# A 16-block transformer kernel on one core: the last stage's first pair of tiles is prepared inside the stage before it

## The chip, the cores and the metric

One core of a Trainium2 chip runs the whole program. The metric is device time in microseconds (us) of one execution; the time before is the median of three runs. The engines are TensorE (PE in the profile, its weight loads PEld), VectorE (DVE), ScalarE (ACT), GpSimd (POOL) and SyncE (SP), which issues most of the DMAs. Each engine works through its own instructions in order, and they meet at semaphores.

## What is computed

The input x is 16 batches of 128 tokens with 256 features. Eight layers update it one after the other; the two that matter here are the last two:

```
x = x + tanh(g_xattn[3]) * L3_xattn(layernorm(x), ctx, ctx)
x = x + tanh(g_ffn[3])   * L3_ffn(layernorm(x))

L3_xattn(Q, K, V):   # per batch, Q, K, V are 128 x 256
    score = sigmoid(Q.T @ K / sqrt(128))      # 256 x 256
    return V @ score

L3_ffn(x):           # router, 8 experts (2 chosen for each token), and a shared part of width 1024
    shared = (silu(x @ sw1.T) * (x @ sw2.T)) @ sw3.T
    scores = sigmoid(x @ router_w.T); the two best of scores + expert_bias, their scores normed to sum 1
    routed = sum over the two of weight * expert(x)
    return shared + routed
```

## The kernel before

x stays in SBUF as `x[:, b]`, b = 0 to 15, a tile of 128 tokens by 256 features each. The program has stages 0 to 7, one for each layer. An engine goes to stage s when `stage_over(eng, s)` lets it: it waits until stage s - 1 has made its last update of x. Stages 2, 4 and 6 count their updates in the semaphore `x_done`, so stage 7 begins when `x_done` has 16 more counts than at the start of stage 6.

**Stage 6** (attention, `s6_dve`, `s6_act`, `s6_pe`, `s6_sp`) has one turn for each tile b. DVE normalises tile b + 2 (`norm`, lines 739, 742, 747; POOL computes the reciprocal deviation between them, lines 755 and 757), subtracts for the low half of a piece of the last stage's weights (`w7l`, line 2770), and updates x (line 2772). PE does the scores of tile b + 1 (line 2796) and then the output of tile b (line 2806). ACT does the sigmoid (line 2782) and the high half of the weights' piece (`w7h`, line 2785). SP loads rows, context and weights two turns ahead. `pipeline` writes the turns out: for DVE, which looks two ahead, turn 0, a hardware loop over turns 1 to 12, and turns 13, 14 and 15 written out; for PE, one ahead, turn 15 alone behind the loop; ACT and POOL have all turns in a loop. In DVE's turns 14 and 15 and in PE's turn 15 nothing is left to normalise or score.

**Stage 7** (feed-forward, `s7_pe`, `s7_act`, `s7_dve`, `s7_pool`) works in pairs of tiles. For each of the 8 pairs b the shared part has 8 units j: PE does `up(b, j)`, 12 matmuls (lines 1665 to 1667), ACT a silu (line 1742), DVE the product (line 1760), and later `down`. Ahead of its units each pair needs a front: `pair_stats` (DVE, lines 1321 and 1325), `pair_rstd` (POOL, lines 755 and 757), `pair_apply` (DVE, line 747, out `xnD`), `pair_transpose` (PE, line 1655, into bank 0), `ff_front_act` (ACT, lines 1342 and 1344: `xnT` and its rounded form `xnTh`), `low_x` (DVE, line 1423: the rest `xnTl`), `pair_logits` (PE, line 1530) and `pair_logits_copy` (DVE, line 1539). The front of pair b + 1 lies between the units of pair b. The front of pair 0 has no units before it: all of it stands ahead of the loop, behind `stage_over(7)`. Routed tokens are written to DRAM by POOL's indirect DMAs, in slots that count the `h` products; after pair 3 come the experts' tiles (`tiles_pe` and its fellows), then pairs 4 to 7.

Of the kernel before, what the change touches and what calls it, by code (L numbers as in the profile page):

```python
# [69 lines left out]
def bass_program(nc, a, out, n_stages=8):  # L70
# [5 lines left out]
    with ctx:  # L76
# [1382 lines left out]
        def pair_xn(n):  # L1459
            return xnD[:, n] if n < HALF else xn[:, n % 2]  # L1460

        def way_pos(n):
            return WAY_PAIRS.index(n)

# [177 lines left out]
        def s7_pe(pe):  # L1642
            F = lambda n: f[7, n]
            MM = nc.tensor.matmul
            UP, DOWN = TOP_E * UNIT, TOP_E * UNIT + 4096

            def pair_transpose(n):
                pe.wait_ge(F("xn").sem, F("xn").at(2 * n + 1, 1))
                if n == 1:
                    pe.wait_ge(F("lg").sem, F("lg").at(0, 1))  # L1650
                elif 2 <= n <= HALF:
                    pe.wait_ge(R7.sem, R7.at((0, 1, 3)[n - 2], 15))
                for c in range(NC):
                    for u in range(2):
                        o = nc.tensor.transpose(bank(0)[:, 256 * c + 128 * u:256 * c + 128 * (u + 1)], pair_xn(n)[:, u, 128 * c:128 * (c + 1)], ident[:])
                o.then_inc(F("xnT_psum").sem, 1)

            def up(b, j):
                pe.wait_ge(F("h").sem, F("h").at(b, j - UP_RING + 1))
                for v in range(2):  # L1660
                    o = bank(2 + j % UP_RING)[:, 256 * v:256 * (v + 1)]
                    for c in range(NC):
                        k = UP + 512 * j + 256 * c + 128 * v
                        wh, wl = w7h[:, k:k + 128], w7l[:, k:k + 128]
                        MM(o, wh, xnTh[:, b % 2, c], start=(c == 0), stop=False)  # L1665
                        MM(o, wh, xnTl[:, b % 2, c], start=False, stop=False)  # L1666
                        t = MM(o, wl, xnTh[:, b % 2, c], start=False, stop=(c == NC - 1))  # L1667
                t.then_inc(F("up").sem, 1)

            def down(b, i):  # L1670
                pe.wait_ge(F("hl").sem, F("hl").at(b, i + 1))
                if i == 0:
                    pe.wait_ge(F("acc").sem, F("acc").at(b, -1))
                k = DOWN + C * i
                wh, wl = w7h[:, k:k + C], w7l[:, k:k + C]
                for u in range(2):
                    o = bank(6 + b % 2)[:, C * u:C * (u + 1)]
                    hh, hl = (h[:, i % 4, T * u:T * (u + 1)] for h in (hTh, hTl))
                    MM(o, hh, wh, start=(i == 0 and u == 0), stop=False, skip_group_check=True)
                    MM(o, hh, wl, start=False, stop=False, skip_group_check=True)  # L1680
                    t = MM(o, hl, wh, start=False, stop=(i == 7), skip_group_check=True)
                t.then_inc(F("y").sem, 1)

            def fronts(b, j):
                n = b + 1
                if n < NB // 2 and j == (5 if n == HALF else 2):
                    pair_transpose(n)
                if n < HALF and j == 3:
                    pair_logits(pe, n)
                if (b, j) in WAY_TRANSPOSE:  # L1690
                    way_transpose(pe, WAY_TRANSPOSE[b, j])
                if (b, j) in WAY_LOGITS:
                    way_logits(pe, WAY_LOGITS[b, j])
                if (b, j) in PLACES:
                    group_places(pe, PLACES[b, j])
                if (b, j) == (3, 4):
                    group_count_pe(pe)

            pair_transpose(0)
            pair_logits(pe, 0)  # L1700
            for b in range(NB // 2):
                pe.wait_ge(F("xnT").sem, F("xnT").at(b, 1))
                pe.wait_ge(F("xnTl").sem, F("xnTl").at(b, 1))
                for j in range(8):
                    up(b, j)
                    if j >= DISTANCE:
                        down(b, j - DISTANCE)
                    elif b % HALF:
                        down(b - 1, 8 - DISTANCE + j)
                    fronts(b, j)  # L1710
                if b % HALF == HALF - 1:
                    for i in range(8 - DISTANCE, 8):
                        down(b, i)
                if b == HALF - 1:
                    tiles_pe(pe, L7)
                    for fl in (L7.t_low, L7.u_h, L7.h_low, L7.d_out):
                        pe.wait_ge(fl.sem, fl.at(N_TILES, 0))

        def s7_act(act):
# [14 lines left out]
                if (b, j) in TANH:  # L1734
                    group_tanh(act, TANH[b, j])

            ff_front_act(7, act, 0, 0)
            for b in range(NB // 2):
                for j in range(8):
                    act.wait_ge(F("up").sem, F("up").at(b, j + 1))  # L1740
# [12 lines left out]
        def s7_dve(dve):  # L1753
# [16 lines left out]
                V.scalar_tensor_tensor(x[:, 2 * p:2 * p + 2], bank(6 + p % 2).rearrange("p (u c) -> p u c", u=2), gates[:, 7:8], x[:, 2 * p:2 * p + 2],  # L1770
                                       ALU.mult, ALU.add).then_inc(F("acc").sem, 1)

            def pair_stats(n):
                ff_stats(7, dve, n, n % 2)

            def pair_apply(n):
                for u in range(2):
                    ln_apply(7, dve, 2 * n + u, 2 * (n % 2) + u, pair_xn(n)[:, u])

            COMBINE = {}  # L1780
            for t in range(NB):
                slot = 8 * HALF + 4 + 8 * t // 5
# [2 lines left out]
            def fronts(b, j):  # L1785
                n = b + 1
                if (b, j) in PAIR_STATS:
                    pair_stats(PAIR_STATS[b, j])
                if n < NB // 2 and j == (4 if n == HALF else 1):
                    pair_apply(n)  # L1790
                if (b, j) in WAY_STATS:
                    way_stats(dve, WAY_STATS[b, j])
                if n < NB // 2 and j == (6 if n == HALF else 3):
# [13 lines left out]
                for t in COMBINE.get((b, j), ()):  # L1807
                    combine7(dve, t)

            pair_stats(0)  # L1810
            pair_apply(0)
            low_x(7, dve, 0, 0)
            pair_logits_copy(dve, 0)
            for b in range(NB // 2):
# [13 lines left out]
                    tiles_dve(dve, L7)  # L1828

        def s7_pool(pool):  # L1830
            rs = rstd_step(7, pool)

            def pair_rstd(n):
                for u in range(2):
                    rs(2 * n + u, 2 * (n % 2) + u)

            pair_rstd(0)
            pair_rstd(1)
            way_rstd(pool, 4)
            way_rstd(pool, 5)  # L1840
            pair_rstd(2)
            group_scatter(pool, 0, (0, 1), SCATTER_AT[0])
            way_rstd(pool, 6)
            group_scatter(pool, 0, (2, 3), SCATTER_AT[0])
            way_rstd(pool, 7)
            pair_rstd(3)
            group_scatter(pool, 1, range(4), SCATTER_AT[1])
            group_scatter(pool, 2, range(4), SCATTER_AT[2])
            pair_rstd(4)
            group_scatter(pool, 3)  # L1850
            for k in range(3):
                pool.wait_ge(y_out[k], L7.stored(N_TILES // 3))
            pool.wait_ge(table_ready, 2 * (TABLE_STEPS + RESULT_STEPS))
            for t in range(NB):
                if t in (1, 7, 12):
                    pair_rstd({1: 5, 7: 6, 12: 7}[t])
                gather(pool, t, got7, combined7)

        def tiles_sp(sp, L):
# [894 lines left out]
        def s6_dve(dve):  # L2754
            F = lambda n: f[6, n]

            def norm(b, s):
                ln_stats(6, dve, b, None, s)
                ln_apply(6, dve, b, s, xn[:, s, 0])

            def first():
                norm(0, 0)
                norm(1, 1)

            def body(p, b, n, s, turn, turn_b):
                if n is not None:
                    dve.wait_ge(F("s_psum").sem, F("s_psum").at(b, 1))
                    norm(n, s)
                dve.wait_ge(F("w7_high").sem, F("w7_high").at(b, 1))
                nc.vector.tensor_tensor(w7l[:, bass.ds(b * W7C, W7C)], w7_raw[:, s], w7h[:, bass.ds(b * W7C, W7C)].bitcast(F32), ALU.subtract).then_inc(F("w7_low").sem, 1)  # L2770
                dve.wait_ge(F("y").sem, F("y").at(b, 1))
                nc.vector.scalar_tensor_tensor(x[:, b], bank(4 + s)[:, 0:C], gates[:, 3:4], x[:, b], ALU.mult, ALU.add).then_inc(x_done.sem, 1)

            pipeline(dve, first, body, lambda p, s: None, ahead=2)

# [11 lines left out]
        def s6_pe(pe):  # L2787
# [11 lines left out]
            def body(p, b, n, s, turn, turn_b):  # L2799
                if n is not None:  # L2800
                    scores(n, 1 - s, turn)
                pe.wait_ge(F(f"ctx_loaded{s}").sem, F(f"ctx_loaded{s}").at(turn_b, 16))
                pe.wait_ge(F("s").sem, F("s").at(b, 1))
                pe.wait_ge(x_done.sem, b + (3 * NB - 1))
# [1 line left out]
                    t = MM(bank(4 + s)[:, 0:C], ctxT[:, s, n], sgm[:, s, n], start=(n == 0), stop=(n == 1))  # L2806
                t.then_inc(F("y").sem, 1)

            pipeline(pe, lambda: scores(0, 0, 0), body, lambda p, s: None)

        c_in = [sem("c_in0"), sem("c_in1")]
# [70 lines left out]
        def _(act):  # L2883
# [14 lines left out]
            for s, prog in enumerate((None, lambda: tiles_act(act, L1), lambda: s2_act(act), lambda: s3_act(act), lambda: s4_act(act),  # L2898
                                      lambda: s5_act(act), lambda: s6_act(act), lambda: s7_act(act))):
                if 0 < s < n_stages:  # L2900
                    stage_over(act, s)
                    if s == 1:
                        act.wait_ge(loaded_later, LOADS_1)
# [60 lines left out]
        def _(pool):  # L2964
# [19 lines left out]
            fetch(0, 0)  # L2984
            fetch(1, 1)
            for s in range(1, n_stages):
                stage_over(pool, s)
                if s == 1:
                    s1_pool(pool, ctx_split(pool, fetch), bias_split, bias_rows)
# [170 lines left out]
```

## Time and profile before

| what | us |
|---|---|
| median of 3 runs | 1343.7 |
| lowest and highest run | 1342.25, 1351.01 |
| the profiled execution | 1340.98 |
| its span, first to last instruction | 1339.2 |
| mean granted TensorE clock | 0.931 of full |

Stage 6 runs from about 1030.8 to 1089.45 on the clock of the profiled span. All times of single instructions below are on that clock. The profiled execution is 1.8 us longer than its span and 2.7 us shorter than the median.

### The profile page before, as it was taken

To read this page: it belongs to the slowest core of one execution; us is meant where nothing else is said; L and a number is where in the kernel's file an instruction comes from. 1 tells how busy PE (TensorE), PEld (TensorE's weight loads), DVE (VectorE), ACT (ScalarE), POOL (GpSimd) and SP (SyncE) were. 2 spreads that over 40 slices of the span, in tenths; PEclk is the share of its full clock that TensorE was granted. 3 is DMA by queue.
4 is the path that set the end of the run, shared out by engine and by line. 5 is a ranking of instruction groups with operands and counts; after the bars stand their busy time and mean duration, and the time that the engine had idled before them with its cause. 6 is when DMAs were issued, how large, how long until landed. Compare 5 with 4: busy or idle time off the path is not lost.

```text
span 1339.2 us, 32909 instructions
## 1 busy us (share of the span) xinstructions
PE 1083.3 (81%) x11717; PEld 832.2 (62%) x11717; DVE 853.1 (64%) x2361; ACT 542.5 (41%) x1049; POOL 507.0 (38%) x1023
## 2 busy tenths in 40 slices
PE   4889898885676588887998799999856569989898
PEld 2566666664575244445666567666644449878798
DVE  2665566565454698975666577777756656555475
ACT  2455454554453477662000132323211644346533
POOL 2444554454884888711001111111313214520261
PEclk8898999898798599998999899999868989989999
DMA  5332223501575455421000000000010630124331
GB/s 181 122 112 69 96 89 127 179 18 36 163 215 178 129 148 145 129 90 64 1 0 0 24 25 16 24 16 23 0 40 4 177 94 32 65 95 152 115 106 64
DMA packets 105784, 112.61 MB, mean 84 GB/s; under 512 B 12548, under 2 KB 95636, under 8 KB 104892
## 3 DMA queue, kind: packets, MB, share of 16 engines
q1 hardware_dynamic: 96732, 88.47, 21.1%
q0 software_dynamic: 8064, 22.06, 5.4%
q8 instruction: 78, 1.28, 0.4%
q10 hardware_dynamic: 864, 0.43, 0.1%
q14 instruction: 46, 0.38, 0.1%
HBM read 66.07 MB, written 44.84 MB: 83 GB/s over the span
## 4 chain that ended last, share of the span: by engine, by line
PE 54%; DVE 17%; issue 10%; ACT 6%; DMA 6%; POOL 3%; SPq 1%; another core or an unknown queue 1%; DVEq 1%; ACTq 0%; POOLq 0%
PE psum L2640 5%; DMA PT<-xs 4%; PE psum L1082 3%; PE psum L2395 2%; DVE mx L852 2%; PE psum L1667 2%; PE psum L1665 2%; ACT ext L2347 2%; PE psum L1666 2%; ACT PT L2338 2%; PE psum L1065 2%; PE psum L1014 2%; PE psum L2380 1%; PE psum L1045 1%; DVE mx L2532 1%
## 5 line engine op out<-in xcount | busy, mean ns | idle before, releaser
L755 POOL TENSOR_SCALAR veps<-mv 128x1 f32<-128x1 f32 x112 | 27.0, 241 | 494.9 <-DVE mv L742 324.8
L852 DVE TENSOR_REDUCE mx<-psum 128x6 f32<-128x960 f32 (+3 forms) x80 | 80.7, 1008 | 77.3 <-PE psum L1050 62.5
L733 POOL DMA_INDIRECT got<-ys,rows_y x64 | 63.9, 999 | 117.9 <-DMA ys<-yt 91.7
L939 ACT ACTIVATE PT<-psum 128x1024 f32<-128x1024 f32 x64 | 65.6, 1025 | 76.6 <-PE psum L1070 76.5
L2298 DVE TENSOR_REDUCE mx<-psum 128x4 f32<-128x1024 f32 x64 | 77.0, 1206 | 19.7 <-PE psum L2369 18.7
L2338 ACT ACTIVATE PT<-psum 128x1024 f32<-128x1024 f32 x64 | 65.5, 1024 | 36.4 <-PE psum L2380 34.7
L1665 PE MATMUL psum<-xnTh,w7h 128*128 128x256 f32 x256 | 76.0, 297 | 1.9 <-issue 1.9
L2640 PE MATMUL psum<-mskp,ident_r 128*128 128x512 f32 x256 | 71.2, 414 | 7.5 <-DVE mx L2532 6.4
L2109 DVE SCALAR_TENSOR_TENSOR x<-psum,cw,x 128x256 f32 (+1 forms) x128 | 53.0, 476 | 36.2 <-PE psum L2057 35.9
L1666 PE MATMUL psum<-xnTl,w7h 128*128 128x256 f32 x256 | 74.0, 289 | 0.6 <-issue 0.6
L1667 PE MATMUL psum<-xnTh,w7l 128*128 128x256 f32 x256 | 73.9, 289 | 0.0
L2395 PE MATMUL psum<-PT,arena 128*32 128x256 f32 x1024 | 70.1, 388 | 0.1
L757 POOL TENSOR_TENSOR rstd<-veps,minus_half 128x1 f32<-128x1 f32 x112 | 64.2, 573 | 9.3
L2592 ACT ACTIVATE PT<-psum 128x1024 f32<-128x1024 f32 x32 | 32.9, 1032 | 84.2 <-PE psum L2705 84.2
L1742 ACT ACTIVATE sil<-psum 128x256 f32<-128x256 f32 x64 | 24.7, 386 | 94.6 <-PE psum L1667 81.7
L2054 PE MATMUL psum<-w3h,xnTh 128*128 128x512 f32 x128 | 62.8, 490 | 0.0
L1760 DVE TENSOR_TENSOR hTf<-sil,psum 128x256 f32<-128x256 f32 x64 | 26.8, 418 | 55.1 <-ACT sil L1742 41.2
L2640 PEld LDWEIGHTS psum<-mskp,ident_r 128*128 128x128 f32 x256 | 44.7, 189 | 27.1 <-DVE mx L2532 16.5
L747 DVE TENSOR_SCALAR xn<-x,mv,rstd 128x256 f32 (+1 forms) x88 | 38.0, 440 | 33.9 <-POOL rstd L757 33.8
L1895 PE MATMUL psum<-ident,PT 128*128 128x128 f32 x156 | 33.4, 297 | 26.9 <-DMA PT<-xs 25.7
L2007 DVE TENSOR_TENSOR ht<-silt,psum 128x128 f32<-128x128 f32 x78 | 22.4, 288 | 45.9 <-ACT silt L1977 45.9
L2055 PE MATMUL psum<-w3l,xnTh 128*128 128x512 f32 x128 | 51.5, 403 | 0.0
(412 smaller groups left out, 3425.6 us busy)
## 6 DMA issues: line engine op xcount, KB each, us to landing
xs<-qpad SPq DMA_DIRECT2D x17, 1024.0 KB
PT<-xs SPq DMA_DIRECT2D x78, 128.0 KB, 2.1
ys<-yt SPq DMA_DIRECT2D x78, 128.0 KB, 2.2
ctxT<-in_ctxT SPq DMA_DIRECT2D x48, 128.0 KB
ext<-qscr SPq DMA_DIRECT2D x96, 64.0 KB
w_raw<-in_w SPq DMA_DIRECT2D x16, 384.0 KB, 3.4
arena<-in_w SPq DMA_DIRECT2D x4, 1280.0 KB, 10.0
q_parts<-kscr SPq DMA_DIRECT2D x66, 64.0 KB
```

Of the source, the lines that this page charges most:

```text
L733: pool.indirect_dma_start(out=dst[:, t % 4, k], out_offset=None, in_=ys[:], in_offset=bass.IndirectOffsetOnAxis(ap=rows_y[:, t, k:k + 1], ...
L757: nc.gpsimd.tensor_tensor(rstd[:, s], veps[:, s], minus_half[:], ALU.pow).then_inc(F("rstd").sem, 1)
L852: V.tensor_reduce(mx0[:, u0:u0 + m].rearrange("p j e -> p e j"), src, axis=AX.X, op=ALU.max, negate=True).then_inc(F("mx").sem, 1)
L939: A.activation(PT[:, 1024 * r:1024 * (r + 1)], bank(6, 2), ACT.Exp).then_inc(F("p").sem, 1)
L1665: MM(o, wh, xnTh[:, b % 2, c], start=(c == 0), stop=False)
L1666: MM(o, wh, xnTl[:, b % 2, c], start=False, stop=False)
L1667: t = MM(o, wl, xnTh[:, b % 2, c], start=False, stop=(c == NC - 1))
L2054: MM(o, xh, wh, start=(c == 0), stop=False)
L2298: V.tensor_reduce(mx2[:, k // 2, 4 * (k % 2):4 * (k % 2) + 4], bank(4 - 4 * (k % 2), 2).rearrange("p (h l) -> p h l", h=4), axis=AX.X, op= ...
L2338: nc.scalar.activation(PT[:, 1024 * k:1024 * (k + 1)], bank(6, 2), ACT.Exp, scale=0.25).then_inc(F("p").sem, 1)
L2395: t = MM(bank(2 + s)[32 * m:32 * (m + 1), C * what:C * (what + 1)], g, PT[:, 1024 * k + 256 * m:1024 * k + 256 * (m + 1)], start=(k == 0 a ...
L2640: MM(bank(4 + r), ident_r[:], mskp[:, s, which, part].unsqueeze(1).to_broadcast([128, 4, T]), start=(part == 0), stop=False, skip_group_ch ...
```

## The change

The front of pair 0 moves into the last turns of stage 6, all but `low_x` and `pair_logits_copy`, which stay where they were.

- DVE: `pair_stats(0)` behind the x update of turn 13; `pair_apply(0)` at the head of turn 14.
- POOL: `pair_rstd(0)` ahead of `stage_over(7)`.
- PE: `pair_transpose(0)` at the head of turn 15, ahead of that turn's output matmuls; `pair_logits(0)` behind them, ahead of `stage_over(7)`.
- ACT: `ff_front_act(7, 0, 0)` ahead of `stage_over(7)`.
- The small statistics buffers of stage 7 change sides, so that pair 0 has slots 2 and 3 of the four, where stage 6 uses 0 and 1: slot (n + 1) % 2 in place of n % 2.

```
+        def pair_slot(n):
+            return (n + 1) % 2
+
+        def pair_stats(dve, n):
+            ff_stats(7, dve, n, pair_slot(n))
...
# s7_pe
-            pair_transpose(0)
-            pair_logits(pe, 0)
# s7_act
-            ff_front_act(7, act, 0, 0)
# s7_dve
-            pair_stats(0)
-            pair_apply(0)
             low_x(7, dve, 0, 0)
             pair_logits_copy(dve, 0)
# s7_pool
-            pair_rstd(0)
-            pair_rstd(1)
+            pair_rstd(pool, 1)
...
# s6_dve, body
                     norm(n, s)
+                if n_stages > 7 and isinstance(b, int) and b == NB - 2:
+                    pair_apply(dve, 0)
                 dve.wait_ge(F("w7_high").sem, F("w7_high").at(b, 1))
...
                 nc.vector.scalar_tensor_tensor(x[:, b], bank(4 + s)[:, 0:C], gates[:, 3:4], x[:, b], ALU.mult, ALU.add).then_inc(x_done.sem, 1)
+                if n_stages > 7 and isinstance(b, int) and b == NB - 3:
+                    dve.wait_ge(x_done.sem, 3 * NB + 2)
+                    pair_stats(dve, 0)
# s6_pe, body
                 if n is not None:
                     scores(n, 1 - s, turn)
+                elif n_stages > 7:
+                    pair_transpose(pe, 0)
...
-            pipeline(pe, lambda: scores(0, 0, 0), body, lambda p, s: None)
+            pipeline(pe, lambda: scores(0, 0, 0), body, lambda p, s: None if n_stages == 7 else pair_logits(pe, 0))
# ACT's block
                 if 0 < s < n_stages:
+                    if s == 7:
+                        ff_front_act(7, act, 0, 0)
                     stage_over(act, s)
# POOL's block
+                if s == 7:
+                    pair_rstd(pool, 0)
                 stage_over(pool, s)
```

## Rows read from the trace of the kernel before

**Rows 1.** The page: busy time by engine, and the chain that ended last by engine.
```profile
PE 1083.3 (81%) x11717; PEld 832.2 (62%) x11717; DVE 853.1 (64%) x2361; ACT 542.5 (41%) x1049; POOL 507.0 (38%) x1023
...
PE 54%; DVE 17%; issue 10%; ACT 6%; DMA 6%; POOL 3%; SPq 1%; another core or an unknown queue 1%; DVEq 1%; ACTq 0%; POOLq 0%
```

**Rows 2.** Windows (length; busy PE, PEld, DVE, ACT, POOL; clock; DMA): stage 6, gap.
```profile
1030.80:1089.45 58.65, 34.50 (x128) 24.84 (x128) 35.56 (x80) 32.90 (x40) 12.45 (x32) 0.94 0.53 157
1089.45:1097.10 7.65, 2.75 (x12) 2.38 (x13) 2.53 (x7) 2.36 (x3) 1.56 (x4) 0.56 0.00 1
```

**Rows 3.** Timeline of stage 6's turns 13 to 15: start, us, engine, what.
```profile
1082.78 0.95 DVE L2770 TENSOR_TENSOR w7l<-w_raw,w7h 128x768 fp32r<-128x768 f32 x1
1083.65 0.48 DVE L2772 SCALAR_TENSOR_TENSOR x<-psum,gates,x 128x256 f32<-128x256 f32 x1
...
1084.96 0.96 DVE L2770 TENSOR_TENSOR w7l<-w_raw,w7h 128x768 fp32r<-128x768 f32 x1 [0.83 <-ACT w7h L2785]
...
1086.85 0.48 DVE L2772 SCALAR_TENSOR_TENSOR x<-psum,gates,x 128x256 f32<-128x256 f32 x1 [0.94 <-PE psum L2806]
1087.22 0.83 ACT L2785 CAST w7h<-w_raw 128x768 f32 x1 [0.64 <-DMA w_raw<-in_w]
...
1087.49 1.13 PE L2806 MATMUL psum<-PT,ctxT 128*128 128x256 f32 x4 [0.68 <-DMA ctxT<-in_ctxT]
1088.09 0.96 DVE L2770 TENSOR_TENSOR w7l<-w_raw,w7h 128x768 fp32r<-128x768 f32 x1 [0.75 <-ACT w7h L2785]
1088.97 0.48 DVE L2772 SCALAR_TENSOR_TENSOR x<-psum,gates,x 128x256 f32<-128x256 f32 x1
```

**Rows 4.** Timeline from stage 6's end to pair 0's first silu.
```profile
1089.48 0.75 DVE L1321 BATCH_NORM_STATS2 stats<-x 128x6 f32<-128x256 f32 x2
...
1092.57 0.41 DVE L747 TENSOR_SCALAR xnD<-x,mv,rstd 128x256 f32<-128x256 f32 x1 [0.45 <-POOL rstd L757]
...
1093.13 1.08 PE L1655 MATMUL psum<-ident,xnD 128*128 128x128 f32 x4 [4.51 <-DVE xnD L747]
...
1094.79 0.59 ACT L1344 CAST xnTh<-psum 128x512 fp32r<-128x512 f32 x1
1095.40 1.28 ACT L1742 ACT_TABLE_LOAD   x1
1095.42 0.69 DVE L1423 TENSOR_TENSOR xnTl<-xnT,xnTh 128x512 fp32r<-128x512 f32 x1 [2.43 <-ACT xnTh L1344]
...
1095.44 1.87 PE L1530 MATMUL psum<-wr,xnT 128*128 128x8 f32 x8 [1.22 <-ACT xnTh L1344]
...
1097.16 0.56 PE L1665 MATMUL psum<-xnTh,w7h 128*128 128x256 f32 x1
...
1100.11 0.38 ACT L1742 ACTIVATE sil<-psum 128x256 f32<-128x256 f32 x1 [3.42 <-PE psum L1667]
```

**Rows 5.** Windows of 2 us: length, PE busy (instructions), granted clock, DMA share, GB/s.
```profile
1088.00:1090.00 2.00, 0.62 (x3) 1.00 0.00 0
1090.00:1092.00 2.00, 0.00 (x0) 0.58 0.01 4
...
1100.00:1102.00 2.00, 2.00 (x17) 0.86 0.04 8
```

**Rows 6.** Timeline in pair 0's units: the same kinds of work later.
```profile
1101.80 0.38 ACT L1742 ACTIVATE sil<-psum 128x256 f32<-128x256 f32 x1 [1.31 <-PE psum L1667]
...
1103.23 0.38 ACT L1742 ACTIVATE sil<-psum 128x256 f32<-128x256 f32 x1 [0.76 <-PE psum L1667]
...
1104.21 0.66 PE L1655 MATMUL psum<-ident,xnD 128*128 128x128 f32 x4 [1.01 <-DVE xnD L747]
...
1106.82 0.95 PE L1530 MATMUL psum<-wr,xnT 128*128 128x8 f32 x8
```

**Rows 7.** Timeline at stage 6's start: POOL's first step, PE's first output.
```profile
1031.72 0.22 POOL L755 TENSOR_SCALAR veps<-mv 128x1 f32<-128x1 f32 x1 [6.46 <-DVE mv L742]
...
1037.13 1.91 PE L2806 MATMUL psum<-PT,ctxT 128*128 128x256 f32 x4
```

More of the change, by code:

```diff
@@ L1460, in pair_xn, with pair_apply, pair_rstd, pair_transpose @@
             return xnD[:, n] if n < HALF else xn[:, n % 2]
+        def pair_slot(n):
+            return (n + 1) % 2
+        def pair_stats(dve, n):
+            ff_stats(7, dve, n, pair_slot(n))
+        def pair_apply(dve, n):
+            for u in range(2):
+                ln_apply(7, dve, 2 * n + u, 2 * pair_slot(n) + u, pair_xn(n)[:, u])
+        def pair_rstd(pool, n):
+            rs = rstd_step(7, pool)
+            for u in range(2):
+                rs(2 * n + u, 2 * pair_slot(n) + u)
+        def pair_transpose(pe, n):
+            F = lambda k: f[7, k]
+            pe.wait_ge(F("xn").sem, F("xn").at(2 * n + 1, 1))
+            if n == 1:
+                pe.wait_ge(F("lg").sem, F("lg").at(0, 1))
+            elif 2 <= n <= HALF:
+                pe.wait_ge(R7.sem, R7.at((0, 1, 3)[n - 2], 15))
+            for c in range(NC):
+                for u in range(2):
+                    o = nc.tensor.transpose(bank(0)[:, 256 * c + 128 * u:256 * c + 128 * (u + 1)], pair_xn(n)[:, u, 128 * c:128 * (c + 1)], ident[:])
+            o.then_inc(F("xnT_psum").sem, 1)
         def way_pos(n):
@@ L1645, in s7_pe @@
             UP, DOWN = TOP_E * UNIT, TOP_E * UNIT + 4096
[L1647 to L1656, printed above, removed]
             def up(b, j):
@@ L1686, in fronts @@
                 if n < NB // 2 and j == (5 if n == HALF else 2):
-                    pair_transpose(n)
+                    pair_transpose(pe, n)
                 if n < HALF and j == 3:
@@ L1771, in add_shared @@
                                        ALU.mult, ALU.add).then_inc(F("acc").sem, 1)
[L1773 to L1778, printed above, removed]
             COMBINE = {}
@@ L1787, in fronts @@
                 if (b, j) in PAIR_STATS:
-                    pair_stats(PAIR_STATS[b, j])
+                    pair_stats(dve, PAIR_STATS[b, j])
                 if n < NB // 2 and j == (4 if n == HALF else 1):
-                    pair_apply(n)
+                    pair_apply(dve, n)
                 if (b, j) in WAY_STATS:
@@ L1830, in s7_pool @@
         def s7_pool(pool):
[L1831 to L1835, printed above, removed]
-            pair_rstd(0)
-            pair_rstd(1)
+            pair_rstd(pool, 1)
             way_rstd(pool, 4)
             way_rstd(pool, 5)
-            pair_rstd(2)
+            pair_rstd(pool, 2)
             group_scatter(pool, 0, (0, 1), SCATTER_AT[0])
@@ L1845, in s7_pool @@
             way_rstd(pool, 7)
-            pair_rstd(3)
+            pair_rstd(pool, 3)
             group_scatter(pool, 1, range(4), SCATTER_AT[1])
             group_scatter(pool, 2, range(4), SCATTER_AT[2])
-            pair_rstd(4)
+            pair_rstd(pool, 4)
             group_scatter(pool, 3)
@@ L1855, in s7_pool @@
                 if t in (1, 7, 12):
-                    pair_rstd({1: 5, 7: 6, 12: 7}[t])
+                    pair_rstd(pool, {1: 5, 7: 6, 12: 7}[t])
                 gather(pool, t, got7, combined7)
```

## The prediction, made before the changed kernel ran

> **What bounds the kernel now.** The page comes first [rows 1]: PE is busy for 81% of the span and holds 54% of the chain that ended last, and no other engine holds more than 17% of it. So the kernel is one long PE program with holes in it, and a change pays by the hole it closes. The windows by stage show the hole that this change is about [rows 2]: between stage 6's last update of x and the first `up` matmul of stage 7 lie 7.65 us in which PE is busy for only 2.75, at a mean granted clock of 0.56, and the DMA share is 0.00, so nothing there waits for memory. The timeline says what fills it [rows 4]: one dependent chain across four engines, stats at 1089.48, `xnD` done at 1092.98, transposes at 1093.13, `xnTh` done at 1095.38, logits from 1095.44, first `up` at 1097.16, its silu at 1100.11. Each step waits for the one before.
>
> What ends stage 6 is another chain [rows 3]: the last piece of the last stage's weights lands, ACT makes `w7h` of it (1087.22 to 1088.05), DVE `w7l` (1088.09 to 1089.05), and the update of x behind it in DVE's order ends at 1089.45. DVE waited 0.83, 0.94 and 0.75 us in these turns and PE's last output waited 0.68 us for its context. So turns 14 and 15 have room, but it is cut in pieces, and the front's steps have to be laid against it one by one.
>
> **The change part by part.** Pair 0's tiles, x[:, 0] and x[:, 1], have their last update in turns 0 and 1, so only places in queues hold the front back.
>
> *DVE and POOL, turn 13.* The stats follow the update at 1083.65, as they followed the one at 1088.97 before: there they began 0.51 us after its start [rows 3, 4], so here at 1084.16. From stats to the end of the second `xnD` took 1092.98 - 1089.48 = 3.50 us, POOL's four steps included, and POOL has had nothing to do since the `xn` ahead of 1082.78. The same 3.50 gives `xnD` complete at 1087.66. SP waits for nothing of DVE behind turn 13's `w7l`, which is ahead of the stats, so the loads keep their times.
>
> *What is queued behind that on DVE.* `pair_apply(0)` is a wait for POOL at the head of turn 14. Behind it stand `w7l` of piece 14, the update of x[:, 14], `w7l` of piece 15 and the update of x[:, 15], for which all engines wait. Back to back, DVE's starts overlap the end before by 0.08 (`w7l` at 1082.78 for 0.95, update at 1083.65). So, behind the `xnD` that ends at 1087.66: `w7l` at 1087.58, update at 1088.45, `w7l` at 1088.85, update at 1089.73, ending at 1090.21. Before it ended at 1089.45, so the wait costs stage 6 **0.8 us**. If POOL is no slower than before, that is the whole cost; if the waits were fully hidden it would be 0, if the 3.5 us chain had a further 0.5 us of waking up in it, 1.3.
>
> *PE, turn 15.* The transposes start 1093.13 - 1092.98 = 0.15 us behind `xnD`: 1087.8. The 2 us window that holds PE's last work before the gap has a granted clock of 1.00 [rows 5], and at that clock the four transposes took 0.66, not 1.08 [rows 4, 6]. They end at 1088.45. The output matmuls of tile 15 (1.13 us [rows 3]) ran at 1087.49 before and now run to 1089.55; the update that needs them is due at 1089.73 anyway, so this delay is covered by DVE's, with 0.2 us to spare. Without that cover it would cost the same us for us.
>
> *ACT.* `xnTh` was complete 2.25 us after the transposes' start [rows 4]; with transposes shorter by 0.42 that is 1.83, so 1089.6. ACT's last `w7h` ends at 1088.05, ahead of the first copy at 1088.5. The logits (0.95 us for eight [rows 6]) run from 1089.65 to 1090.6. The load of the silu table (1.28 us) runs behind the copies and ends before the first silu is ready, whichever side of `stage_over` it takes.
>
> *What is late next.* `low_x` stays behind `stage_over(7)`: 1090.25 to 1090.94 (0.69 us [rows 4]). It ends after the logits, so `up(0, 0)` is let go by `xnTl`, at **1091.0** where it was 1097.16: **6.1 us** earlier. That is 6.9 us of front hidden less the 0.8.
>
> *The clock.* PE ran at 1.2 GHz through its first `up` unit, because it had done nothing from 1088.62 to 1093.13: the granted clock fell from 1.00 within the window 1090 to 1092 and came back within that of 1100 to 1102 [rows 5]. Twelve matmuls took some 12 x 0.213 = 2.56 us there; two silus at full clock are 1.43 us apart for the same twelve [rows 6]. In the changed kernel PE's idle pieces from turn 14 on are about 0.9, 0.1 and 0.4 us; a turn of stage 6 had (58.65 - 34.50) / 16 = 1.5 us of idle on average at a mean clock of 0.94 [rows 2], and it stood at 1.00 at the stage's end [rows 5]. PE's share of busy time there was 0.59, and from 1087.8 to 1091.0 it is 2.7 of 3.2. So I take the full clock for the first units: another 2.56 - 1.43 = **1.1 us**. The first silu then comes at 1091.0 + 1.43 + (2.95 - 2.56) = 1092.8 instead of 1100.11.
>
> The Trainium skill ("TensorE: Matmul & The Clock Gate", What's actually happening) says that the throttled clock is the default and activity releases it; this trace agrees at 1090 and at 1100. The same section warns that the place where the clock rises varies from run to run; by that the 1.1 us would be anything from a little below 0 to 1.5, which the range holds anyway.
>
> *Everything behind.* Units, fronts of later pairs, POOL's scatters (their slots count `h`) and the experts' tiles are released by stage 7's own progress; no DMA reaches the stage ahead of them. So the shift is carried to the end. The other slots of the small buffers cost nothing: same instructions, same distance. **Sum: 6.1 + 1.1 = 7.2 us**, 1340.98 to 1333.8 for the profiled execution. That execution is 2.7 us below the median of its kind; against the median, 1343.7 - 7.2 = **1336.5**.
>
> **The rivals.** *Half clock.* PE's work in the last two turns is thin and the clock falls before or in the front. Against it: the windows of stage 6 at 1.00. For it: the fall at 1090 to 1092 came at most 3.4 us after PE's last matmul, and at stage 6's start the same output took 1.91 us at the low level [rows 7]. Then transposes to 1088.9, output to 1090.8, update to 1091.3, logits 1090.8 to 1092.7, first `up` at about 1092.5 and silu 2.95 later, at 1095.4: gain 4.7, time 1339.0.
>
> *The gain is given back later.* The chain after pair 0 holds some steps on DVE and POOL; if a transfer or a POOL sequence not tied to stage 7's start set the tiles' begin, the shift would end there. I found none. Gain 0 to 3, time 1341 to 1343.7. The same times hold if the change does not do what it says, for instance if ACT or PE reach their moved steps late and the front runs where it did.
>
> *Slower.* One mechanism: POOL. DVE now waits for POOL's square roots with the end of stage 6 queued behind it, so each us that POOL is late past 1087.1 makes stage 6 a us longer. It decides from 7.2 us late on, that is if POOL delivers after 1094.3; at 15 us late the kernel would be 0.6% slower, 1351. POOL stands right behind the exit of its loop there. At stage 6's start, too, it stood behind a loop's exit, and its wait of 6.46 us was ended by DVE's `mv`, by nothing of its own [rows 7], and it has some 2 us of slack between 1082.8 and the first `mv`. That makes this unlikely.
>
> The Trainium skill ("Runtime: NRT & Kernel Launch", Instruction fetch mechanics) says that a taken branch to code outside the fetched window stalls the engine for a DMA fetch. That speaks for this rival, on PE and ACT too, since all three now do front work right behind a loop; the page gives no duration, and this trace shows no such stall at a loop's exit.
>
> **How the numbers follow.** Forecast as worked out (gain 6 to 8.5): 0.66. Half clock or a smaller stall, gain 3.5 to 6: 0.18. Given back or not done, gain 0 to 3.5: 0.08. More than 8.5, if later holes shrink too: 0.05. Slower: 0.03. What a measurement of this kernel can tell from no change is about 1%, 13.4 us, and nothing here but the far end of the last case reaches it: faster by over 1% 0.02, within 1% 0.96, slower by over 1% 0.02. The range takes in gains from 2 to 8.5 against the median and, since the three runs differ by some us (1342.25 to 1351.01), some more on the low side: 1331.5 to 1342.
>
> **What would show it.** In the changed profile: stats of line 1321 right behind turn 13's update; `xnD` complete some 1.8 us ahead of stage 6's end; that end 0.8 us later relative to turn 13; first `up` about 7.4 us after turn 13's update began, where it was 13.5; granted clock 1.00 through the first units; `xnTl` as the releaser of the first `up`. Wrong would be: a POOL or ACT step that starts late with nothing to wait for, a clock at 0.5 there, or tiles that begin no earlier.

## The result, and the profile after

Twenty executions of each kernel, on the chips on which both ran: before 1348.73 us median (1342.25 to 1355.33), after 1342.34 us (1330.99 to 1350.82). The ratio is **0.9958**, 95% interval 0.9940 to 0.9975, so the change saves 5.7 us (3.4 to 8.1); the two medians alone lie 6.4 apart. The three runs of before that the prediction started from had a median of 1343.7; seventeen more moved it up by 5 us. The ratio is therefore what is to be compared with the forecast, 7.2 of 1343.7 or 0.9946. That lies inside the interval, so the timing alone can't tell a gain of 7.2 us from one of 5.7; the traces can. The absolute time lies 0.3 us outside the range.

The profiled execution after took 1345.8 us (span 1344.0), more than the one before. What the change did has to be read around its place, and the rest of the span on its own (below). The page, as [rows 1]:

```profile
PE 1088.5 (81%) x11717; PEld 836.7 (62%) x11717; DVE 853.0 (63%) x2361; ACT 542.5 (40%) x1049; POOL 510.0 (38%) x1023
...
PE 53%; DVE 17%; issue 11%; ACT 6%; DMA 5%; POOL 3%; another core or an unknown queue 2%; SPq 1%; DVEq 1%; ACTq 0%; POOLq 0%
```

The windows of stage 6 and of the hole behind it, as [rows 2]. The hole was 7.65 us long at a clock of 0.56; it is 0.98 us at 1.00:

```profile
1031.00:1090.21 59.21, 35.35 (x138) 25.78 (x138) 37.01 (x86) 33.98 (x42) 14.07 (x36) 0.94 0.53 155
1090.21:1091.19 0.98, 0.41 (x4) 0.35 (x4) 0.78 (x3) 0.00 (x0) 0.00 (x0) 1.00 0.00 0
```

The timeline of turns 13 to 15 and of the first unit, as [rows 3] and [rows 4]:

```profile
1083.78 0.48 DVE L2771 SCALAR_TENSOR_TENSOR x<-psum,gates,x 128x256 f32<-128x256 f32 x1
...
1084.18 0.74 DVE L1321 BATCH_NORM_STATS2 stats<-x 128x6 f32<-128x256 f32 x2
...
1087.28 0.41 DVE L747 TENSOR_SCALAR xnD<-x,mv,rstd 128x256 f32<-128x256 f32 x1 [0.45 <-POOL rstd L757]
...
1087.61 0.95 DVE L2769 TENSOR_TENSOR w7l<-w_raw,w7h 128x768 fp32r<-128x768 f32 x1
...
1087.74 0.66 PE L1486 MATMUL psum<-ident,xnD 128*128 128x128 f32 x4 [0.93 <-DVE xnD L747]
...
1088.24 1.03 PE L2810 MATMUL psum<-PT,ctxT 128*128 128x256 f32 x4
...
1088.92 0.59 ACT L1344 CAST xnTh<-psum 128x512 fp32r<-128x512 f32 x1
...
1089.56 1.06 PE L1557 MATMUL psum<-wr,xnT 128*128 128x8 f32 x8 [0.30 <-ACT xnTh L1344]
1089.73 0.48 DVE L2771 SCALAR_TENSOR_TENSOR x<-psum,gates,x 128x256 f32<-128x256 f32 x1
1090.25 0.69 DVE L1423 TENSOR_TENSOR xnTl<-xnT,xnTh 128x512 fp32r<-128x512 f32 x1
...
1091.19 0.36 PE L1681 MATMUL psum<-xnTh,w7h 128*128 128x256 f32 x1 [0.57 <-DVE xnTl L1423]
...
1092.94 1.28 ACT L1755 ACT_TABLE_LOAD   x1 [3.43 <-issue]
...
1094.23 0.66 ACT L1755 ACTIVATE sil<-psum 128x256 f32<-128x256 f32 x2
```

Counted from turn 13's update, the lines down to the first `up` matmul are where the prediction put them within 0.25 us, but for PE's last output: it ended 0.4 us earlier than forecast, at 1089.27, and so 0.46 us before the update that needs it began. The surprise is the last two lines. In [rows 4] the load of the silu table ran at 1095.40, right behind the copies, long before the first silu was due. Now ACT stands idle for 3.43 us and loads the table at 1092.94, when the first `up` unit is done, so the first silu waits 1.3 us for it.

To compare traces I measure from the start of turn 13's update of x: to the first `up` 13.5 us before and 7.4 after, to the first silu 16.5 and 10.45.

### The profile page after: what moved, and what is told of

Same layout as the page of the kernel before. It is cut to its first block, busy times and chain, and to the rows that moved or that the text cites. A ratio compares the mean times of both kernels' runs of the same rounds, so it can differ in the third digit from the quotient of the medians.

```text
span 1344.0 us, 32909 instructions
## 1 busy us (share of the span) xinstructions
PE 1088.5 (81%) x11717; PEld 836.7 (62%) x11717; DVE 853.0 (63%) x2361; ACT 542.5 (40%) x1049; POOL 510.0 (38%) x1023
## 3 DMA queue, kind: packets, MB, share of 16 engines
q8 instruction: 78, 1.28, 0.4%
## 4 chain that ended last, share of the span: by engine, by line
PE 53%; DVE 17%; issue 11%; ACT 6%; DMA 5%; POOL 3%; another core or an unknown queue 2%; SPq 1%; DVEq 1%; ACTq 0%; POOLq 0%
PE psum L2637 5%; DMA PT<-xs 4%; PE psum L1082 3%; PE psum L2392 3%; ACT PT L2335 2%; DVE mx L852 2%; PE psum L2377 2%; PE psum L1065 2%; PE psum L1681 2%; PE psum L1137 2%; PE psum L1045 2%; POOL rstd L757 1%; DVE mx L2529 1%; PE psum L1683 1%
## 5 line engine op out<-in xcount | busy, mean ns | idle before, releaser
L2637 PEld LDWEIGHTS psum<-mskp,ident_r 128*128 128x128 f32 x256 | 44.4, 188 | 27.1 <-DVE mx L2529 16.5
L1681 PEld LDWEIGHTS psum<-xnTh,w7h 128*128 128x128 f32 x256 | 50.6, 198 | 3.3 <-issue 3.2
L1682 PEld LDWEIGHTS psum<-xnTl,w7h 128*128 128x128 f32 x256 | 50.9, 199 | 1.5 <-issue 1.5
```

Of the source, the lines that this page charges most:

```text
L2637: MM(bank(4 + r), ident_r[:], mskp[:, s, which, part].unsqueeze(1).to_broadcast([128, 4, T]), start=(part == 0), stop=False, skip_group_ch ...
```

## Why the table load moved, and first tests

ACT's instructions in the built programs show the reason, with the semaphores that each waits for. A lone WAIT is an instruction that only waits:

```
before:  WAIT           for xnT_psum        after:  COPY xnT       waits xnT_psum
         COPY xnT       waits x_done                CAST xnTh
         CAST xnTh                                  WAIT           for h, up
         WAIT           for h                       ACT_TABLE_LOAD
         ACT_TABLE_LOAD                             ACTIVATE sil   waits x_done
         ACTIVATE sil   waits up
```

Theory A is that this costs 1.3 us and everything else went as worked out. The rivals are a chance delay of ACT, a shift that is not carried on, and other prices for the parts. Ten more runs were made, on chips on which the kernel before takes about 1325 us and not 1349. Ratios are to the kernel before on the same chip.

**The changed kernel again.**

> The changed kernel once more. The measure taken from every trace is the stretch from the start of turn 13's update of x to the start of the first silu of stage 7: 16.46 us before, 10.45 in the first trace of the changed kernel. Theory A (the front is hidden as worked out, and the silu's table load, which now waits for the first up, gives 1.3 us of it back): 10.4 to 10.6 again, first up 7.4 to 7.6 after the update, table load directly ahead of the silu; time 5 to 7 us under before. Rival B (the table load stood there by chance, for instance by a late fetch of ACT's instructions): the load's start differs from the first trace's, and the stretch may be 9.1.

Ratio 0.9956 (0.9941 to 0.9970). First up at 7.41, table load at 9.15, first silu at 10.44 us after the update, to 0.01 us where they were on the other chip. Chance is out.

**The table load set free.**

```
                     if s == 7:
                         ff_front_act(7, act, 0, 0)
-                    stage_over(act, s)
+                    else:
+                        stage_over(act, s)
```

> ACT no longer waits for stage 6 itself in stage 7 (its first silu waits for the first up, which waits for stage 6 on PE). Theory A: the first silu then has two waits instead of three, the load of its table keeps only the one that is long fulfilled, runs behind xnTh at some 5.9 us after turn 13's update, and the first silu starts 9.1 to 9.2 us after the update instead of 10.45; first up unchanged at 7.4. Time some 1.3 us under the changed kernel, too little for the timing to show alone. Rival B: load and silu where they were, 10.45.

Its timeline (the update of turn 13 began at 1071.93):

```profile
1077.07 0.59 ACT L1344 CAST xnTh<-psum 128x512 fp32r<-128x512 f32 x1
1077.68 1.28 ACT L1755 ACT_TABLE_LOAD   x1
...
1079.35 0.36 PE L1681 MATMUL psum<-xnTh,w7h 128*128 128x256 f32 x1 [0.57 <-DVE xnTl L1423]
...
1081.05 0.38 ACT L1755 ACTIVATE sil<-psum 128x256 f32<-128x256 f32 x1 [2.09 <-PE psum L1683]
```

The WAIT now holds `h` alone. The load is back behind `xnTh`, the first `up` is unchanged at 7.42, the first silu comes at 9.12 as expected. The ratio, 0.9962 (0.9945 to 0.9980), can't show 1.3 us, and does not.

**The same wait put on the kernel before.**

```
                 for j in range(8):
+                    if b == 0 and j == 0:
+                        act.wait_ge(x_done.sem, 4 * NB)
                     act.wait_ge(F("up").sem, F("up").at(b, j + 1))
```

> The kernel before, with one more wait ahead of the first silu (the end of stage 6, long fulfilled by then), so that three waits stand there as in the changed kernel. Theory A: the table load moves behind the first up; the stretch from turn 13's update to the first silu grows from 16.46 to 17.7, time 1.3 us over before. Rival B: no change, the load stays right behind xnTh.

Its ACT timeline (update at 1071.91):

```profile
1083.06 0.59 ACT L1344 CAST xnTh<-psum 128x512 fp32r<-128x512 f32 x1
1088.41 1.28 ACT L1744 ACT_TABLE_LOAD   x1 [4.76 <-issue]
1089.70 0.38 ACT L1744 ACTIVATE sil<-psum 128x256 f32<-128x256 f32 x1
```

First silu at 17.79 instead of 16.46: 1.33 us from one wait that was long fulfilled: the WAIT ahead of the load holds `h` and `up` here. Ratio 1.0023 (1.0008 to 1.0038), which is 1.1 to 5.0 us more than before; 1.33 lies inside. Both directions show the mechanism: theory A holds.

## The other terms, one by one

**The clock alone.** PE is kept at work in the hole of the kernel before; nothing else moves.

```
+            for k in range(24):
+                nc.tensor.transpose(bank(1)[:, 0:128], ident[:], ident[:])
             pair_transpose(0)
+            for k in range(8):
+                nc.tensor.transpose(bank(1)[:, 0:128], ident[:], ident[:])
             pair_logits(pe, 0)
```

> The kernel before, with PE kept at work in the hole by transposes of the identity into a free bank (24 ahead of pair 0's transposes, 8 behind them); results are not touched. Theory (the half clock cost the front and the first units 2.4 us: 0.4 in the transposes, 0.9 in the logits, 1.1 in the first up unit): granted clock 1.00 throughout, stretch from turn 13's update to the first silu 16.46 - 2.4 = 14.0 us, time 2 to 3 us under before. Rival (the clock falls all the same, or the dummy work delays the transposes): 16.5 or more.

Timeline (update at 1075.61):

```profile
1081.51 2.84 PE L1700 MATMUL psum<-ident 128*128 128x128 f32 x24 [0.89 <-DVE x L2776]
...
1085.06 0.66 PE L1655 MATMUL psum<-ident,xnD 128*128 128x128 f32 x4 [0.71 <-DVE xnD L747]
...
1089.56 0.38 ACT L1746 ACTIVATE sil<-psum 128x256 f32<-128x256 f32 x1 [1.38 <-PE psum L1667]
```

Transposes 0.66 instead of 1.08, first silu at 13.95: the half clock was worth 2.5 us of the hole, against 2.4 expected. The timing gives 1.000 (0.9981 to 1.0019), which hardly admits 2.5 us (0.9981): that this gain reaches the end of the program is not shown by the timing; see the part on what came of the lead.

**Half of the change.** DVE's and POOL's steps stay in stage 6; transposes, copies and logits are put back at the head of stage 7, and ACT's wait for the stage ahead of its copies.

```
-                elif n_stages > 7:
-                    pair_transpose(pe, 0)
...
+            pair_transpose(pe, 0)
+            pair_logits(pe, 0)
             for b in range(NB // 2):
                 pe.wait_ge(F("xnT").sem, F("xnT").at(b, 1))
...
+            ff_front_act(7, act, 0, 0)
             for b in range(NB // 2):
```

> Half of the change: only DVE's and POOL's steps of pair 0's front are in stage 6, transposes, copies and logits are back behind the stage's end. Theory: they begin when the last update ends, some 6.5 us after turn 13's update, without the 3.6 us of normalisation; stage 6 ends no later than in the changed kernel. PE is idle for only 1.3 us before, so the clock stays at 1.00: transposes at 6.5, xnTh at 8.4, logits to 9.3, first up at 9.1, first silu 10.9. At half clock it would be 6.6, 8.9, 10.6 and 13.6. Without the change's PE and ACT part the gain is then 5.6 (or 2.9) of the 7.3 us that hiding everything would give.

The windows of PE (length, busy, granted clock):

```profile
1076.00:1078.00 2.00, 0.44 (x3) 0.94 0.00 0
1078.00:1080.00 2.00, 0.99 (x4) 0.50 0.00 0
```

First silu at 13.49. I had expected the full clock and 10.9; this is the half-clock branch (13.6): PE stood idle for 1.56 us before its transposes, and the clock fell. Ratio 0.9971 (0.9953 to 0.9989). So the rival of the half clock was near. The length of an idle piece alone does not decide it, though: in the kernel with the clock alone changed PE stood idle for 1.66 us in turn 14, ahead of its scores, and the clock stayed at 1.00. In the full change the early transposes went with a clock that stayed up; the half of the change on DVE and POOL alone gains 3.0 of the 7.3 us.

**POOL made late.** Six more powers ahead of pair 0's, 3.1 us of work.

```
                 if s == 7:
+                    pool.wait_ge(f[7, "mv"].sem, f[7, "mv"].at(0, 1))
+                    plain(pool)
+                    for k in range(6):
+                        P.tensor_tensor(th[:, 0, k:k + 1], mv[:, 2, 1:2], minus_half[:], ALU.pow)
                     pair_rstd(pool, 0)
```

> The changed kernel with six more powers of 0.57 us on POOL ahead of pair 0's deviations (into a small buffer that is free), 3.4 us in all. Theory (each us that POOL is late is a us of stage 6, since DVE's wait for it has the rest of the stage queued behind it): pair 0's second xnD 3.4 us later, last update of stage 6 3.4 us later, first silu 13.8 us after turn 13's update instead of 10.45, time 2 to 3 us under before instead of 5 to 7. Rival (slack takes part of it up): less than 2 us on the first silu.

Timeline (update at 1070.75):

```profile
1072.46 3.13 POOL L2997 TENSOR_TENSOR th<-mv,minus_half 128x1 f32<-128x1 f32 x6 [2.94 <-DVE mv L1325]
...
1077.33 0.41 DVE L747 TENSOR_SCALAR xnD<-x,mv,rstd 128x256 f32<-128x256 f32 x1 [0.45 <-POOL rstd L757]
...
1078.70 1.91 PE L2810 MATMUL psum<-PT,ctxT 128*128 128x256 f32 x4
...
1080.65 0.48 DVE L2771 SCALAR_TENSOR_TENSOR x<-psum,gates,x 128x256 f32<-128x256 f32 x1 [0.79 <-PE psum L2810]
```

`xnD` and the transposes come 3.1 us later, the last update 3.95 us later (at 9.90 instead of 5.95): more than us for us, because PE, idle meanwhile for 3.98 us, fell to the half clock and its last output took 1.91 us. The first silu is at 14.39, 3.95 later. Ratio 0.9985 (0.9968 to 1.0002). The price of the slower rival is right, or a little low; its condition was absent: POOL was not late in any trace.

**DVE's order.** The low weights of piece 14 go ahead of the normalisation (with the free load).

```
-                if n_stages > 7 and isinstance(b, int) and b == NB - 2:
-                    pair_apply(dve, 0)
                 dve.wait_ge(F("w7_high").sem, F("w7_high").at(b, 1))
                 nc.vector.tensor_tensor(w7l[:, bass.ds(b * W7C, W7C)], ...)
+                if n_stages > 7 and isinstance(b, int) and b == NB - 2:
+                    pair_apply(dve, 0)
```

> As the kernel with the free load, and DVE does piece 14 of the low weights ahead of pair 0's normalisation, in the time in which it waited for POOL. Theory A (DVE's queue behind the wait for POOL sets the end of stage 6, 0.8 us later than it could be): stage 6's last update ends about 0.4 us earlier, the first up starts 0.3 to 0.5 us earlier, at 7.0 after turn 13's update, then held by the logits; first silu at 8.7. Rival: PE's order (transposes ahead of the last output) sets the end, and nothing moves: 9.1.

Timeline (update at 1071.07):

```profile
1072.45 0.93 DVE L2767 TENSOR_TENSOR w7l<-w_raw,w7h 128x768 fp32r<-128x768 f32 x1
...
1072.79 0.67 POOL L755 TENSOR_SCALAR veps<-mv 128x1 f32<-128x1 f32 x1 [2.96 <-DVE mv L1325]
...
1075.48 0.66 PE L1486 MATMUL psum<-ident,xnD 128*128 128x128 f32 x4 [1.34 <-DVE xnD L747]
...
1077.04 0.48 DVE L2771 SCALAR_TENSOR_TENSOR x<-psum,gates,x 128x256 f32<-128x256 f32 x1 [0.36 <-PE psum L2810]
```

The last update stays at 5.97, first silu 9.15, ratio 0.9957 (0.9942 to 0.9973): no gain. The rival's number came, but not by its mechanism. PE's order does not set the end of the stage in the changed kernel, where PE's last output was done 0.46 us before the last update began. Here POOL's first step took 0.67 us where it took 0.22, with DVE's two-input operation beside it. `xnD`, the transposes and PE's last output all came 0.45 us later, and the last update waited 0.36 us for that output. An estimate from these rows: without POOL's 0.45 us the update would have begun at about 5.5, the 0.4 us earlier that was expected. By this estimate DVE's order was the limit, as theory A of this run says, and the new order lost on POOL what it gained on DVE. The Trainium skill ("SBUF — State Buffer", SBUF: two separate sides) describes this: a VectorE operation with two SBUF inputs and a GpSimd operation that reads SBUF exclude each other for the whole instruction. The trace agrees: 0.67 against 0.22, and POOL's step ends 0.08 us after DVE's operation.

**The front begun earlier.** Pair 0's stats go into turn 13's wait for POOL, ahead of its update (with the free load).

```
-                    norm(n, s)
+                    if n_stages > 7 and isinstance(b, int) and b == NB - 3:
+                        ln_stats(6, dve, n, None, s)
+                        dve.wait_ge(x_done.sem, 3 * NB + 2)
+                        pair_stats(dve, 0)
+                        ln_apply(6, dve, n, s, xn[:, s, 0])
+                    else:
+                        norm(n, s)
...
-                if n_stages > 7 and isinstance(b, int) and b == NB - 3:
-                    dve.wait_ge(x_done.sem, 3 * NB + 2)
-                    pair_stats(dve, 0)
```

> As the kernel with the free load, with pair 0's stats moved from behind turn 13's update into that turn's own wait for POOL (between stats and normalisation of tile 15, 1.1 us in which DVE stood idle). Theory A (DVE's wait for POOL and PE's transposes ahead of the last output cost stage 6 0.6 us, because the front began only behind the update): POOL is done before turn 14 begins, DVE waits for nothing there, transposes at 3.2 us after turn 13's update instead of 3.96, last update at 5.3 as before the change, first up at 6.9 instead of 7.4, first silu at 8.5 instead of 9.1. Rival: the stats push tile 15's normalisation back, its scores and sigmoid follow, and the end of stage 6 is later: 9.5 or more.

Last update at 5.40, first `up` at 6.86: both as expected. But the clock fell after all, as the windows say (update at 1070.60, first `up` at 1077.46):

```profile
1075.00:1077.00 2.00, 1.54 (x12) 1.00 0.00 0
1077.00:1079.00 2.00, 1.71 (x9) 0.54 0.00 0
```

The first silu came at 9.80, not 8.5; ratio 0.9956 (0.9935 to 0.9976). 9.80 lies where the rival had it (9.5 or more), but not by the rival's cause: stage 6 ended as early as expected, and the half clock took the rest. PE had been busy for 1.54 of the 2 us before, more than in stage 6's average turn, and still the clock dropped; so the mean busy share, by which the prediction argued, does not decide this.

**`xnTl` in stage 6 as well.** On top of the stats in the wait, `low_x` goes ahead of DVE's last update.

```
-            low_x(7, dve, 0, 0)
             pair_logits_copy(dve, 0)
...
+                if n_stages > 7 and isinstance(b, int) and b == NB - 1:
+                    low_x(7, dve, 0, 0)
                 dve.wait_ge(F("y").sem, F("y").at(b, 1))
```

> As the kernel with the stats in the wait, and pair 0's xnTl as well in stage 6, ahead of DVE's last update of x. Theory: what then lets the first up go is the end of stage 6 itself or the logits, not xnTl: last update later by up to 0.6 us (0.69 us of work in front of it), first up within 0.2 us of the update's end, at 6.4 to 6.6; first silu 8.1 to 8.3; time 7 to 9 us under before. Rival: the wait for xnTh pushes the last update back by more than it saves, first up at 7.0 or later.

Last update at 6.06, first `up` at 6.59, first silu at 8.32: the shortest of all, 8.1 us less than before. Ratio 0.9961 (0.9938 to 0.9985). The clock stayed up here (update at 1072.83, first `up` at 1079.42), with PE hardly busier than in the kernel with the stats in the wait:

```profile
1075.00:1077.00 2.00, 1.61 (x10) 1.00 0.50 190
1077.00:1079.00 2.00, 1.55 (x11) 1.00 0.00 0
```

## What came of the lead further on

**The kernel before again**, for its trace on such a chip and for what the timing shows of no change:

> The kernel before, unchanged, as a run of its own: what the timing shows where nothing differs, and its trace on a chip whose executions take some 1325 us instead of 1345. Expected: ratio 1.000 within its interval; stretch from turn 13's update to the first silu 16.46 again; from the first silu on, the same distances as the changed kernel's second trace (first to seventeenth silu 41.5, to the experts' first tile 90) if the shift is carried whole; if some of it is given back behind the first units, its stretches there are shorter than those of the changed kernel.

Ratio 0.9999 (0.9978 to 1.0020). The stretches from turn 13's update, in us, from the traces; the last column is the difference of the measured ratio from 1, times 1325 us. "Before" is this run, "the change" its second trace. The rows POOL late, warm and half are from another chip than the rest, with no trace of the kernel before:

| kernel | first silu | 17th silu (pair 2) | experts' first tile | end of span | timed, us |
|---|---|---|---|---|---|
| before | 16.5 | 58.2 | 107.0 | 250.2 | -0.1 |
| before, load late | 17.8 | 59.1 | 107.7 | 250.2 | +3.0 |
| POOL late | 14.4 | 55.6 | 104.2 | 247.0 | -2.0 |
| before, warm | 14.0 | 55.2 | 103.9 | 248.0 | 0.0 |
| half of the change | 13.5 | 55.2 | 103.8 | 247.1 | -3.8 |
| the change | 10.4 | 52.0 | 100.6 | 245.0 | -5.8 |
| stats in the wait | 9.8 | 51.1 | 99.6 | 243.9 | -5.8 |
| apply later | 9.2 | 50.4 | 99.1 | 244.0 | -5.7 |
| load free | 9.1 | 50.4 | 99.0 | 244.0 | -5.0 |
| xnTl too | 8.3 | 49.6 | 98.0 | 244.1 | -5.2 |

Every lead at the first silu is still whole at the experts' first tile, some 90 us later: 6.1 us becomes 6.4 for the change. The delay of the load-late row is not: 1.3 us becomes 0.7. In the changed kernel the load's 1.3 us is carried (52.0 against 50.4); there the next pair's stats stand behind the first product. So the rival of a shift that is given back in pairs 0 to 3 is refuted. Behind the tiles' start the leads of 6 to 9 us end at 5.2 to 6.3. The warm kernel's span ends 2.2 us ahead, while its timing shows 0.0 with some 2.5 us either way. The windows of the tiles' stretch and of pairs 4 to 7 show where (columns as in [rows 2]). The kernel before again:

```profile
1180.52:1243.45 62.93, 59.08 (x449) 53.74 (x448) 33.97 (x117) 41.27 (x148) 0.00 (x0) 0.99 0.47 147
1249.65:1317.07 67.42, 65.95 (x554) 65.36 (x554) 45.87 (x117) 23.98 (x67) 36.07 (x44) 1.00 0.28 87
```

The kernel with `xnTl` too:

```profile
1170.82:1237.02 66.20, 60.10 (x449) 55.10 (x448) 34.19 (x117) 41.87 (x149) 0.00 (x0) 0.97 0.44 140
1241.81:1310.18 68.37, 65.62 (x554) 65.02 (x553) 45.96 (x117) 23.97 (x67) 36.45 (x44) 1.00 0.28 86
```

The kernel with the free load, pairs 4 to 7 alone:

```profile
1239.29:1309.20 69.91, 67.14 (x554) 66.55 (x553) 45.84 (x117) 23.98 (x68) 36.21 (x44) 0.98 0.28 84
```

The same instructions take 62.9 us at 0.99 and 66.2 at 0.97; pairs 4 to 7 take 67.4 at 1.00 and 69.9 at 0.98. A part of it goes with where the clock falls. Whether a bigger lead makes it fall worse there, or each trace drew its own place, one trace of each kernel can't say; nor can the timings, whose intervals are 4 to 6 us wide. That stays open, and with it whether any of the four further kernels is better than the change: none is by its timing.

**The first chip.** There the profiled span after was 4.8 us longer than before, though the first silu came 6 us sooner after turn 13's update. The view of waits has lines for ACT that no trace of the other chips has, with no known releaser (us in total, times, longest). After:

```profile
ACT sil L1755 <- remote: 14.8, 5, 5.1
ACT xnT L1342 <- remote: 3.3, 1, 3.3
```

Before:

```profile
ACT sil L1742 <- remote: 10.7, 3, 3.9
```

The experts' first tile came at 109.0 before and 108.8 after. The lead was lost mostly between the last silu of pair 3 and the first tile: that piece took 6.2 us before at the full clock, and 11.2 after, of which some 10 at half clock by the windows' granted clock. Before, then after:

```profile
1186.50:1192.67 6.17, 3.49 (x25) 2.85 (x25) 2.78 (x6) 1.82 (x6) 0.00 (x0) 1.00 0.29 85
1181.31:1192.53 11.22, 7.12 (x30) 6.17 (x31) 5.89 (x14) 1.85 (x7) 0.00 (x0) 0.54 0.25 68
```

Behind it the waits add up: from the first tile to the end 151.4 us against 146.5. Over 20 executions the lead is there; in one pair of profiles it is hidden. What these waits are was not found.

## Why the prediction was off

- **The order of the steps and their durations**: right, but for PE's last output (above). Counted from turn 13's update, measured (forecast): `xnD` complete 3.91 (4.01), transposes 3.96 (4.15), last update ended 6.43 (6.56), `xnTl` from 6.47 (6.60), first `up` 7.41 (7.35), released by `xnTl`. PE took 0.25 us from `xnTl`'s end to the first `up`, where I had allowed 0.06.
- **The 0.8 us on stage 6**: nearly. The last update began 5.95 us after turn 13's, 5.32 before: 0.63.
- **The clock**: right, 1.00 throughout, and the price right by a run of its own. The argument for it was weak, and there was luck in it: half of the change and the kernel with earlier stats lost the full clock with idle pieces and busy shares that differ little.
- **"The load of the silu table runs behind the copies and ends before the first silu is ready, whichever side of `stage_over` it takes"**: this step failed. I asked on which side of one wait the load would stand, not how many waits the first silu would then have. With three waits the load stood behind the first `up` unit in all four traces, with two it ran early in all eight; the pairs that differ by that alone show 1.3 us (10.44 against 9.12, 17.79 against 16.46). The sum becomes 7.2 - 1.3 = 5.9 us; the first silu came 6.0 us sooner in the traces, and the timing shows 5.7. That is in the band of 3.5 to 6 us that the prediction gave a chance of 0.18, by the smaller stall and not by the half clock.
- **"So the shift is carried to the end"**: shown up to the experts' tiles on the later chips; behind them the leads of 6 to 9 us lose 1 to 3 us, with part of it at the half clock. Why is open.
- **The base**: 1343.7, the median of three runs, was taken as the time to subtract from, and the range left 0.3 us for its spread on the high side (1343.7 less the smallest gain of 2 is 1341.7, the bound 1342). Twenty runs gave 1348.73, 5.0 us more; three runs from 1342 to 1351 had already shown such a spread. With the base of 20 runs the forecast would have read 1341.5, against 1342.34. It took both errors to leave the range: without the load's 1.3 us the time would have been some 1341.0, and with the right base the range would have reached to 1347.

## What to carry to other kernels

When work is moved ahead of a stage's wait, count the waits that the next instruction on that engine now has, and look at what stands in front of it in the built program: a table load there may end up behind the wait for the very data it should be loaded ahead of. Dropping a wait that another one implies is the cure. To begin a front early pays a second time through the clock, but two kernels here that differed little from the change lost that again, and neither PE's idle piece nor its busy share told which would. A change of 0.4% is judged by the ratio and by stretches between two marks in the traces; spans of single profiles differed by more than the change.

## Not expected of the hardware

- The table load took 1.28 us, with the silu 1.29 us behind the load's start wherever the silu was due (four traces). The Trainium skill ("ScalarE: Activation LUTs", What ACT_TABLE_LOAD costs) gives 1283 ns for the load, as the trace, and some 1380 ns of drain besides; no trace here shows a drain. The silu starts as the load ends, and with the free load the load itself starts 0.02 us behind ACT's copy.
- POOL's small step took 0.67 us instead of 0.22, and its power 1.13 instead of 0.57 in the kernel with the stats in the wait, beside a two-input DVE operation.
- The granted clock fell behind 2 us in which PE was busy for 1.54, and stayed at 1.00 behind 2 us with 1.07 (the changed kernel, from 1086).
- The kernel before took 1348.73 us in the median of the first measurement and 1324 to 1325 in all three later ones.
